# Graph layer with residual and layer norm: the last column group in runs of 256, 128 and 128 columns, a new order of the last steps, stores of two row tiles

## The reference

```python
def _gcn_layer(x, adj, W, b):
    d_inv_sqrt = (jnp.sum(adj, axis=1) + 1e-09) ** (-0.5)
    msg = d_inv_sqrt[:, None] * adj * d_inv_sqrt[None, :] @ x
    return jax.nn.relu(msg @ W + b)
...
    H_f = _gcn_layer(feature_x, adj, W_f, b_f)
    H_s = _gcn_layer(spatial_x, adj, W_s, b_s)
    H_cat = jnp.concatenate([H_f, H_s], axis=1)
    attn = jax.nn.sigmoid(H_cat @ W_att + b_att)
    return attn * H_f + (1.0 - attn) * H_s
...
x = _layernorm(x + _L0_gnn_ref(x, L0_gnn_spatial_x, adj, ...), axis=-1)
```

## Time and profile before

| what | value |
|---|---|
| median of 3 runs | 394.38 us (394.3 to 394.52) |
| the profiled execution, its time | 394.35 us |
| its span in the trace | 392.6 us |
| PE busy | 376.2 us (96%) |
| DVE busy | 303.9 us (77%) |
| ACT busy | 283.8 us (72%) |
| POOL busy | 161.8 us (41%) |

### The profile page before, as it was taken

The page is one execution under the profiler, slowest core; times in us unless marked ns, Lnnn a source line. Parts: engine busy times, 40 slices in busy tenths (PEclk is TensorE's granted clock), DMA queues, the critical chain, the costliest instruction groups (busy, mean ns, idle before and its releaser), DMA issues. The chain is left out here.

```text
span 392.6 us, 5474 instructions
## 1 busy us (share of the span) xinstructions
PE 376.2 (96%) x1778; PEld 314.7 (80%) x1778; DVE 303.9 (77%) x434; ACT 283.8 (72%) x364; POOL 161.8 (41%) x199
## 2 busy tenths in 40 slices
PE   7779999999999999999999999999999999999990
PEld 7668778778888888888888888888788888888990
DVE  2889996979668875959589593929977887888896
ACT  3777788788878887887868887878633566668464
POOL 2343601770067603782259200010000427787764
PEclk9999999999999999999999999999999999999996
DMA  7999999999999999999999999999575434354001
GB/s 276 424 416 423 419 419 424 418 422 419 422 417 422 425 417 423 417 422 422 419 422 419 414 416 421 417 416 390 222 276 191 192 124 187 126 194 122 28 28 54
DMA packets 24508, 130.77 MB, mean 333 GB/s; under 512 B 2848, under 2 KB 7840, under 8 KB 10400
## 3 DMA queue, kind: packets, MB, share of 16 engines
q1 hardware_dynamic: 24480, 130.43, 82.6%
HBM read 128.32 MB, written 2.10 MB: 332 GB/s over the span
## 5 line engine op out<-in xcount | busy, mean ns | idle before, releaser
L398 PE MATMUL sums<-Ah,Yh 128*128 128x512 f32 (+1 forms) x528 | 203.7, 386 | 5.4 <-DVE Yl L503 5.0
L400 PE MATMUL sums<-Al,Yh 128*128 128x512 f32 (+1 forms) x528 | 202.1, 383 | 0.0
L399 PE MATMUL sums<-Ah,Yl 128*128 128x512 f32 (+1 forms) x528 | 202.1, 383 | 0.0
L494 DVE TENSOR_TENSOR Al<-raw,Ah 128x2048 fp32r<-128x2048 f32 (+2 forms) x86 | 159.5, 1861 | 32.2 <-ACT Ah L690 32.2
L690 ACT ACTIVATE Ah<-raw 128x2048 fp32r<-128x2048 f32 (+2 forms) x86 | 125.8, 1475 | 50.4 <-DMA raw<-in_At 31.5
L398 PEld LDWEIGHTS sums<-Ah,Yh 128*128 128x128 f32 x528 | 99.2, 188 | 27.3 <-DVE Yl L503 6.6
L400 PEld LDWEIGHTS sums<-Al,Yh 128*128 128x128 f32 x528 | 99.2, 188 | 19.6
L399 PEld LDWEIGHTS sums<-Ah,Yl 128*128 128x128 f32 x528 | 99.3, 188 | 19.0
L700 ACT ACTIVATE nat<-nat 128x2048 f32<-128x2048 f32 (+1 forms) x54 | 100.1, 1854 | 19.8 <-DMA nat<-in_adj 19.1
L514 DVE TENSOR_TENSOR acc<-sums,acc 128x512 f32<-128x512 f32 (+1 forms) x122 | 78.3, 675 | 36.6 <-PE sums L400 36.6
L840 POOL TENSOR_TENSOR S<-S,raw 128x512 f32<-128x512 f32 x40 | 69.2, 1730 | 27.5 <-DMA raw<-in_At 24.3
(11 more groups left out here) (51 smaller groups left out, 135.7 us busy)
## 6 DMA issues: line engine op xcount, KB each, us to landing
raw<-in_At SPq DMA_DIRECT2D x63, 1024.0 KB, 9.0
nat<-in_adj SPq DMA_DIRECT2D x47, 1024.0 KB, 11.6
nat<-in_adj SPq DMA_DIRECT2D x8, 768.0 KB, 9.4
xs<-in_xs SPq DMA_DIRECT2D x7, 512.0 KB, 10.4
out<-xs SPq DMA_DIRECT2D x32, 64.0 KB, 1.6
nat<-in_adj SPq DMA_DIRECT2D x2, 512.0 KB, 6.9
raw<-in_At SPq DMA_DIRECT2D x2, 512.0 KB, 8.3
xs<-in_xs SPq DMA_DIRECT2D x2, 128.0 KB, 7.0
```

Of the source, the lines that this page charges most:

```text
L398: pe.matmul(to, Yh[:, t % YRING, hs], high, start=first, stop=False)
L399: pe.matmul(to, Yl[:, t % YRING, hs], high, start=False, stop=False)
L400: mm = pe.matmul(to, Yh[:, t % YRING, hs], low, start=False, stop=last)
L494: dve.tensor_tensor(Al[:, k % SPLITS, a * IB:b * IB], raw[:, k % RAWS, a * IB:b * IB], Ah[:, k % SPLITS, a * IB:b * IB], ALU.subtract).the ...
```

## The change

The last group's second run of 256 columns becomes two of 128 columns (tiles 30 and 31 apart), which share the item K-1. The last steps of DVE, ACT and POOL are put in a new order, tiles 26 and 27 are mixed by POOL, tile 31 by DVE; tiles 28 and 29 are normalised by ACT. DVE's `join_last` is split: statistics are a step `spread_last`. SP stores rows 0 to 29 in pairs, one DMA for each pair.

```diff
-    runs.append((G - 1, s6 + s7, 2, (0, IB // 2)))
-    runs.append((G - 1, s6 + s7, 0, (IB // 2, IB)))
+    runs.append((G - 1, s6 + s7, 2, (0, 2 * P)))
+    runs.append((G - 1, s6 + s7, 0, (2 * P, 3 * P)))
+    runs.append((G - 1, s6 + s7, 1, (3 * P, IB)))
...
-    order += [(G - 1, s6 + s7), (G, s6 + s7)]
     items.extend([(first + g, t) for t in s] for g, s in order)
+    items.append([(first + G - 1, t) for t in s6 + s7])
+    items.append([(first + e, t) for e in (G, G + 1) for t in s6 + s7])
...
-    HALVES = [range(LAST, LAST + 2), range(LAST + 2, T)]
-    OWN_MIX = [LAST - 2, LAST - 1, T - 2]
-    BY_VECTOR = [*HALVES[0], T - 2, T - 1]
+    LAST_ROWS = [range(LAST, LAST + 2), range(T - 2, T - 1), range(T - 1, T)]
+    PAIR = LAST_ROWS[0]
+    OWN_MIX = [T - 2, T - 1]
...
-            for r in [*range(LAST), *BY_VECTOR]:
-                if r < LAST:
-                    sp.wait_ge(norm_ok, r + 1)
+            stores = [range(r, r + 2) for r in range(0, T - 2, 2)] + LAST_ROWS[1:]
+            for rows in stores:
+                a, b = rows[0], rows[-1] + 1
+                if b <= T - 2:
+                    sp.wait_ge(norm_ok, b)
                 else:
-                    sp.wait_ge(last_norm_ok, BY_VECTOR.index(r) + 1)
-                sp.dma_start(out_v[r], xs[:, r, 0:F]).then_inc(stored, 16)
-            sp.wait_ge(stored, 16 * T)
+                    sp.wait_ge(last_norm_ok, b - (T - 2))
+                sp.dma_start(out_p[:, a:b, :], xs[:, a:b, 0:F]).then_inc(stored, 16)
+            sp.wait_ge(stored, 16 * len(stores))
...
-                    if k == K - 1 and step == GT:
-                        weigh_half(HALVES[0])
+                    if k == K - 1 and step == 2 * GT:
+                        weigh_last(0)
+                    if k == K - 1 and step == 6 * GT:
+                        weigh_last(1)
...
-            weigh_half(HALVES[1])
+            weigh_last(2)
...
-            for r in of_group(TAIL - 2):
+            for r, q in zip(of_group(TAIL - 2), of_group(TAIL - 1)):
                 join(r)
+                affine(q)
             evacuate_half(FIRST_LAST + TAIL, 0)
...
-            for r in HALVES[0]:
+            for r in PAIR:
+                logit(r)
+            for r in PAIR:
                 join(r)
-            for r in HALVES[1]:
-                affine(r)
-                logit(r)
+            affine(T - 2)
+            logit(T - 2)
+            evacuate_half(FIRST_LAST + TAIL + 2, 0)
             mix(T - 2)
             join_last(T - 2)
+            evacuate_half(FIRST_LAST + TAIL + 2, 1)
+            spread_last(T - 2)
+            affine(T - 1)
+            logit(T - 1)
+            mix(T - 1)
             join_last(T - 1)
-            for r in BY_VECTOR:
-                normalise_last(r)
+            spread_last(T - 1)
+            normalise_last(T - 2)
+            normalise_last(T - 1)
...
-            for r in HALVES[0]:
+            for r in of_group(TAIL - 1)[1:]:
                 square(r)
-            for r in of_group(TAIL - 1):
+            relu(T - 2)
+            gate([T - 2])
+            for r in PAIR:
+                square(r)
+            for r in of_group(TAIL - 1)[:3]:
+                normalise(r)
+            relu(T - 1)
+            gate([T - 1])
+            for r in [LAST - 1, *PAIR]:
                 normalise(r)
```

More of the change, by code:

```diff
@@ L84, in build @@
     FINAL = K - 2 * G
-    FIRST_LAST = len(runs) - G - 1
+    FIRST_LAST = len(runs) - (G - 1) - 3
     BLK = GT * IB
@@ L190, in build @@
     xs_v = xs_in.rearrange("(m p t f) -> m p t f", p=P, t=GT, f=H2)
-    out_v = out.rearrange("(r p) f -> r p f", p=P)
+    out_p = out.rearrange("(r p) f -> p r f", p=P)
     bf_v = b_f.rearrange("(a h) -> a h", a=1).to_broadcast([P, H])
@@ L420, in weigh, with weigh_last @@
                     weigh_tile(r, 1).then_inc(w_ok, 1)
-            def weigh_half(rows):
-                part = HALVES.index(rows)
-                evacuated = 2 * evac_no[FIRST_LAST + TAIL + part]
+            def weigh_last(n):
+                rows = LAST_ROWS[n]
+                evacuated = 2 * evac_no[FIRST_LAST + TAIL + n]
                 pe.wait_ge(z_ok, rows[0])
@@ L562, in join_last @@
             def join_last(r):
-                n = r - (T - 2)
                 dve.wait_ge(gate_ok, r + 1)
@@ L568, in join_last, with spread_last @@
                                          in1=xs[:, r, 0:F], op0=ALU.mult, op1=ALU.add).then_inc(y_ok, 1)
+            def spread_last(r):
+                n = r - (T - 2)
                 dve.wait_ge(y_ok, r + 1)
@@ L578, in normalise_last @@
             def normalise_last(r):
[L579 to L587, removed]
+                dve.wait_ge(last_rstd_ok, r - (T - 2) + 1)
+                dve.tensor_scalar(xs[:, r, 0:F], xs[:, r, 0:F], mv[:, r, 0:1], rstd[:, r:r + 1],
+                                  ALU.subtract, ALU.mult).then_inc(last_norm_ok, 1)
             def of_group(g):
@@ L658, in _ @@
             evacuate_half(FIRST_LAST + TAIL, 1)
[L659 to L662, removed]
             join(LAST - 4)
-            for r in HALVES[0]:
+            for r in PAIR:
                 affine(r)
-            join(LAST - 3)
-            for r in HALVES[0]:
-                logit(r)
+            for r in of_group(TAIL - 1)[1:]:
+                join(r)
             evacuate_half(FIRST_LAST + TAIL + 1, 0)
             evacuate_half(FIRST_LAST + TAIL + 1, 1)
-            for r in HALVES[0]:
+            for r in PAIR:
+                logit(r)
+            for r in PAIR:
                 join(r)
-            for r in HALVES[1]:
-                affine(r)
-                logit(r)
+            affine(T - 2)
+            logit(T - 2)
+            evacuate_half(FIRST_LAST + TAIL + 2, 0)
             mix(T - 2)
             join_last(T - 2)
+            evacuate_half(FIRST_LAST + TAIL + 2, 1)
[3 more added lines that the diff above has]
+            mix(T - 1)
             join_last(T - 1)
-            for r in BY_VECTOR:
-                normalise_last(r)
+            spread_last(T - 1)
+            normalise_last(T - 2)
+            normalise_last(T - 1)
         @block.scalar
@@ L770, in _ @@
                 normalise(r)
-            for r in of_group(TAIL - 2):
-                square(r)
             for r in of_group(TAIL - 1):
                 relu(r)
+            for r in of_group(TAIL - 2)[:2]:
+                square(r)
             gate(of_group(TAIL - 1))
+            for r in of_group(TAIL - 2)[2:]:
+                square(r)
+            for r in PAIR:
+                relu(r)
             for r in of_group(TAIL - 2):
                 normalise(r)
-            for r in HALVES[0]:
-                relu(r)
             square(LAST - 4)
[L781 to L788, removed]
-                square(r)
-            for r in of_group(TAIL - 1):
+            gate(PAIR)
+            for r in of_group(TAIL - 1)[1:]:
+                square(r)
+            relu(T - 2)
+            gate([T - 2])
+            for r in PAIR:
+                square(r)
+            for r in of_group(TAIL - 1)[:3]:
[3 more added lines that the diff above has]
+            for r in [LAST - 1, *PAIR]:
                 normalise(r)
@@ L860, in deviation @@
                 pool.tensor_tensor(rstd[:, a:b], vare[:, a:b], mhalf[:, 0:b - a], ALU.pow).then_inc(rstd_ok, b - a)
-                if a >= LAST:
-                    return
                 pool.wait_ge(rstd_ok, b)
@@ L892, in of_group @@
                 return range(g * GT, (g + 1) * GT)
-            for g in range(TAIL):
+            for g in range(TAIL - 1):
                 if g >= 1:
@@ L898, in _ @@
                 for r in of_group(g):
-                    if r not in OWN_MIX:
-                        mix(r)
-            mix(HALVES[0][0])
+                    mix(r)
+            mix(LAST - 4)
+            mean(of_group(TAIL - 2))
+            for r in range(LAST - 3, LAST):
+                mix(r)
+            deviation(of_group(TAIL - 2))
+            mix(PAIR[0])
             mean(of_group(TAIL - 1))
-            mix(HALVES[0][1])
-            mean(HALVES[0])
+            mix(PAIR[1])
+            mean(PAIR)
             deviation(of_group(TAIL - 1))
-            mix(T - 1)
-            deviation(HALVES[0])
+            deviation(PAIR)
             last_deviation([T - 2])
```

## The result

The changed kernel takes 396.45 us (median of 5 runs, 396.38 to 396.52), the kernel before 394.52 us beside it (5 runs, 394.3 to 394.64). The ratio is 1.005, with a 95% interval of 1.0036 to 1.0065: 0.5% slower. The profiled execution took 396.45 us and its span is 394.7 us, 2.1 us longer than before.

What follows compares the result with a forecast made beforehand. PE's gapless stream to the last matmul, then a 10.48 us tail of waits, bounds the kernel. Span 392.6 + 5.70 (stream) - 2.04 (tail) - 1.09 (stores) = 395.2, time 396.9 us, 0.65% slower; whole range 393.5 to 398.4.

Steps and rivals of the forecast that it cites:

- The stream: PE's stream in item K-1: 96 narrow matmuls plus tile 30's weighing start the last matmul at 387.82, 5.70 us later.
- p: Distance of two fp32r matmuls of 128 columns in item K-1, taken as 0.114 us, since each still changes its weights.
- the 0.76 of the prediction: PE's stream sum in us would be this much less if the skill page's load time replaced 0.114.
- 81 ns: Skill page's load-and-matmul pair, not taken: last matmul at 384.7, time 393.8 us; part of the hidden-load rival's chance.
- The load is hidden: Rival: PE overlaps loads with streaming, p falls toward 0.065; 392.3 us, up to 392.9 with DVE late; chance 0.17.
- Float32's pace: Rival: fp32r at 128 columns falls to float32's pace, distance 0.228, time 407.8 us; chance 0.11.
- The tail does not shorten: Rival: PE's stream grows as forecast, but tile 31's way waits for ACT or POOL; 398 to 400 us; chance 0.06.
- the forecast: Main case: distance of narrow matmuls between 0.10 and 0.125 us, own range 395.5 to 398.4; chance 0.66.
- No wait inside the item: Item K-1's first weighing moves to step 8, due at 378.3; DVE's evacuation stays near 377, so PE does not wait.
- The cover: Slack between DVE's evacuation of the 256-column run's second half and PE's first weighing: about 1 us.
- The tail: From DVE's last evacuation to the last normalise's end: 4.9 us instead of 6.94, a gain of 2.04.
- The stores: SP's store queue at the end is gone: last normalise to end 2.14 us in place of 3.23, a gain of 1.09.

Runs made afterwards that it cites:

- the two-load kernel: Changed kernel with two matmuls instead of three per block of its last item, 64 loads in place of 96: 394.31 us, ratio to the kernel before 0.9999.
- The bf16 kernel: Changed kernel with the last item's 96 matmuls reading the upper halves of both operands as bf16, same shapes and count: 394.12 us in one run.
- the kernels of 64 columns: Changed kernel with last item's matmuls cut to 64 columns for tile 30 and 32 for tile 31: 399.59 us; or all cut to 64: 399.54 us.

## Why the prediction was right

**The stream.** Forecast: p = 0.114 and the last matmul at 387.82. Measured: 0.1114 and 387.66. The rows of the float32 products and of the column sums pointed the right way and were 5% short: they give 0.106 or 0.107. The 0.114 was a slip that helped: the 1.82 us from 370.79 to 372.61 hold 17 distances and not 16, 0.107 each. With 0.107 the same sum gives 396.3, still near; that 0.114 came out closer is luck. The theory behind the choice was shown: a distance of 0.11 from 192 to 32 columns, 0.057 with 2-byte operands, 3.47 us gone with a third of the loads gone at the same columns, and a first distance of 0.04 to 0.09 that goes by columns. By the Trainium skill, "TensorE: Matmul & The Clock Gate", "LDWEIGHTS (loading the stationary operand)", a load of 128 columns takes 128 / 1.2 = 107 ns, an estimate by its formula; the narrow stream here shows 111. By 107 the sum is 0.67 us less than mine; the 0.76 of the prediction used 0.106. The same page's 81 ns for a sustained pair of load and 128-column matmul, "Back-to-back issue gap", was not seen with fp32r, nor with bf16, which went at 57.

**The rivals.** *The load is hidden* fell: in a stream where each narrow fp32r matmul has its own load none came under 0.11 (the 0.06 of the two-load kernel stand beside wide ones, two loads in 0.23). The bf16 kernel shows besides that its price was set too well. I gave it 392.3 to 392.9; with a distance of 0.057 the time was 394.12, since DVE's work up to the last evacuation did not fit. The prediction named that limit and sized it at 0.6; it was about 2 us (the last evacuation starts at 385.28, 2.28 behind the last matmul in place of 0.31). *Float32's pace* fell with the constant distance. *The tail does not shorten* fell with 4.70 us in place of 6.94. One slip in the chances: the forecast, float32's pace and the tail that does not shorten are all slower, 0.83 together, where I wrote 0.81.

**No wait inside the item.** PE has no wait from 360 us on. The cover was thinner than I said: DVE began the evacuation of the 256-column run's second half at 377.39 and not near 377.0, and the weighing started at 378.40: 0.6 us between the evacuation's end and the weighing, where about 1 was forecast.

**The tail.** From the evacuation to the last normalise's end 4.9 was forecast and 4.70 measured. The affine came after 0.87 (0.9), DVE's mix 0.97 behind it (1.0), from there to the end of the epsilon step 1.80 (1.84), and from that to the last normalise's start 0.71 (0.81). That the way was shortened by DVE's order was shown by moving tile 30's steps back, 2.0 us against 1.7 expected; PE's last weighing is as late, as the prediction said.

**The stores.** From the last normalise to the end 2.14 was forecast and 2.0 measured. The step was right in what the changed kernel shows, a queue that is gone. But the runs part the two causes: in the kernel before pairs bring 0.7 us; in the changed kernel they bring nothing, and it is the spread of the normalises that took the queue away. The prediction booked 1.09 us under the stores without saying which.

**The sum.** Forecast 395.2 of span, measured 394.7: the stream 0.16 less, the chain 0.2 less, the stores 0.1 less. The 0.16 hides two larger differences: counted from the item's own start the stream is 0.36 shorter than forecast (11.89 against 12.25 us, 0.25 of it by the distance), and the item started 0.20 later. The stream cost 5.5 us and the tail gave back 3.4. The sum also took the full clock for granted. That held at 128 columns, and the kernels of 64 columns show that it need not.

## What to carry over

Before a matmul stream is cut into narrower pieces, look up what one weight load costs beside it: where every matmul changed its stationary operand, the stream went no faster than one such load for each (0.11 us for 4 bytes here), and the break-even width is the one that streams as long. I estimate it at some 240 columns, from 0.120 us for 256 columns and 0.111 for a load. A shorter tail has to pay for all the loads that the cut adds: here 48 loads cost 4.9 us when they came alone, the stream of the whole change grew by 5.5 us with tile 30's weighing in it, and the tail gave back 3.4. And a queue of short stores at the end is worth a look by itself: putting them in pairs was a part of the change that, alone, made the kernel before faster.

## What the runs showed of the hardware beyond that

TensorE's granted clock fell from 1.00 to 0.50 (2.4 to 1.2 GHz) in the midst of a stream without a gap, after 8.6 us of fp32r matmuls of 64 columns with a load each, and in the other kernel after 6.2 us of 64 columns and 2.5 of 32 (the 0.9 us of a weighing in either). From then on the matmuls lay 0.21 us apart. In the changed kernel, with 128 columns at the same distance, it stayed at 1.00 to the end of the stream. So a busy share of 1.00 in the profile does not vouch for the clock: its own column has to be read. One run stands behind each of the two kernels in which it fell, and why it fell is not settled.

A DMA of two row tiles (128 x 2 x 128 values) took SP 0.37 us to issue, in the changed kernel's last five stores, no more than the median of 0.43 for one row tile in the kernel before (0.42 in the changed kernel with single stores).
